# Graph network kernel: type-embedding weight products moved to the prologue, biases awaited where used, normalised tiles stored by the synchronisation engine

## The reference

```python
x = _layernorm(x + _L0_gnn_ref(x, W_fc, attn_l, attn_r, W_res, src, dst))
h = jnp.concatenate([x, node_emb[node_type]], axis=-1)        # 768 + 128
def rgcn_conv(h, src, dst, edge_type, w_rel, w_root, bias):
    xw = jnp.einsum('nd,rde->rne', h, w_rel)                   # one matrix for each of 3 relations
    msg = xw[edge_type, src] * inv[dst, edge_type][:, None]    # mean over the edges of a relation
    return jax.ops.segment_sum(msg, dst, num_nodes) + h @ w_root + bias
h = relu(rgcn_conv(h, ..., w_rel1, w_root1, b1))               # and two more, 896->896->768->768
return _layernorm(x + h)
```

## Time and profile before

| | |
|---|---|
| median of 3 runs | 2536.57 us (2536.53 to 2536.61) |
| profiled execution | 2534.83 us, its span in the trace 2533.0 us |
| PE busy | 2204.2 us, 87% of the span |
| DVE, ACT, POOL busy | 49%, 31%, 18% |
| DMA | mean 85 GB/s |

### The profile page before, as it was taken

The page is one execution under the profiler, slowest core; times in us unless marked ns, Lnnn a source line. Parts: engine busy times, 40 slices in busy tenths (PEclk is TensorE's granted clock), DMA queues, the critical chain, the costliest instruction groups (busy, mean ns, idle before and its releaser), DMA issues.

```text
span 2533.0 us, 29974 instructions
## 1 busy us (share of the span) xinstructions
PE 2204.2 (87%) x10953; PEld 1843.8 (73%) x10954; DVE 1230.3 (49%) x1882; ACT 780.5 (31%) x1062; POOL 450.6 (18%) x378
## 2 busy tenths in 40 slices
PE   3997762778878649999999999999999989999997
PEld 1554441233333239999999989999999989999997
DVE  7887657887786453332232342333232342334335
ACT  0133224676677432121121141121221231212212
POOL 0000002787779610000000000000000000000000
PEclk9999885899889869999999999999999999999999
DMA  0133332211011142333243432333323423434332
GB/s 17 45 85 90 90 88 65 69 31 31 16 31 31 51 145 70 100 109 105 88 117 88 110 105 83 97 93 101 116 79 110 120 84 96 118 106 132 104 99 79
DMA packets 138639, 215.04 MB, mean 85 GB/s; under 512 B 87580, under 2 KB 87818, under 8 KB 138513
## 3 DMA queue, kind: packets, MB, share of 16 engines
q1 hardware_dynamic: 99179, 147.28, 20.3%
q0 software_dynamic: 39344, 66.16, 9.0%
HBM read 182.38 MB, written 30.62 MB: 84 GB/s over the span
## 4 chain that ended last, share of the span: by engine, by line
PE 57%; DMA 5%; DVE 2%; ACT 2%; issue 0%; SPq 0%; ACTq 0%; DVEq 0%
PE banks L1101 29%; PE banks L1073 26%; DMA w_raw<-in_L_gnn_w_root_dram 3%; DVE w_lo L1342 1%; ACT w_hi L1221 1%; DMA s_x<-x_tiles 1%; PE banks L1136 0%; PE banks L1110 0%; DMA emb_raw<-in_L_gnn_w_rel_dram 0%; PE banks L1123 0%; PE banks L1154 0%; DVE h_lo L1373 0%; ACT accT L1249 0%; DVE tail_stats L1392 0%; DVE back L1390 0%
## 5 line engine op out<-in xcount | busy, mean ns | idle before, releaser
L1073 PE MATMUL banks<-ct_in,h_hi 125*128 125x416 f32 (+1 forms) x1710 | 604.5, 353 | 0.6 <-ACT accT L1206 0.6
L1073 PE MATMUL banks<-ct_in,h_lo 125*128 125x416 f32 (+1 forms) x1710 | 603.3, 353 | 0.0
L1101 PE MATMUL banks<-g_hi,w_hi 128*128 128x416 f32 (+1 forms) x1440 | 517.1, 359 | 22.0 <-DVE g_lo L1364 22.0
L1101 PE MATMUL banks<-g_lo,w_hi 128*128 128x416 f32 (+1 forms) x1440 | 513.3, 356 | 0.0
L1101 PE MATMUL banks<-g_hi,w_lo 128*128 128x416 f32 (+1 forms) x1440 | 512.5, 356 | 0.0
L1342 DVE TENSOR_TENSOR w_lo<-w_raw,w_hi 128x768 fp32r<-128x768 f32 (+1 forms) x228 | 227.8, 1000 | 467.3 <-ACT w_hi L1221 467.3
L849 PE MATMUL head_sums<-pw,x 125*65 125x512 f32 x720 | 299.1, 564 | 59.1 <-POOL pw L647 49.2
L1221 ACT CAST w_hi<-w_raw 128x768 fp32r<-128x768 f32 (+1 forms) x228 | 197.8, 868 | 450.1 <-PE banks L1101 354.7
L1073 PEld LDWEIGHTS banks<-ct_in,h_lo 125*128 125x128 f32 x1710 | 323.7, 189 | 4.3
L647 POOL TENSOR_TENSOR pw<-y,csum 125x1250 f32<-125x1250 f32 x120 | 313.6, 2658 | 74.3 <-PE head_sums L849 68.8
L1073 PEld LDWEIGHTS banks<-ct_in,h_hi 125*128 125x128 f32 x1710 | 322.5, 189 | 4.1 <-ACT accT L1206 0.8
(11 more groups left out here) (189 smaller groups left out, 1544.3 us busy)
## 6 DMA issues: line engine op xcount, KB each, us to landing
w_raw<-in_L_gnn_w_rel_dram SPq DMA_DIRECT2D x117, 384.0 KB, 3.1
ct_in<-s_ct POOLq DMA_DIRECT2D x18, 2031.2 KB, 28.4
w_raw<-in_L_gnn_w_rel_dram SPq DMA_DIRECT2D x54, 448.0 KB, 3.9
ct_in<-s_ct POOLq DMA_DIRECT2D x9, 2041.0 KB, 28.6
s_ct<-ct_stage SPq DMA_DIRECT2D x30, 610.4 KB
w_raw<-in_L_gnn_w_root_dram SPq DMA_DIRECT2D x39, 384.0 KB, 3.1
w_raw<-in_L_gnn_w_root_dram SPq DMA_DIRECT2D x18, 448.0 KB, 5.7
low_spread<-s_low SPq DMA_DIRECT2D x12, 610.4 KB
```

What stands on the lines that cost most here:

```text
L1073: ins = nc.tensor.matmul(pb[0:rows, PA, 0:s.w], a, b, start=j == 0, stop=j == len(pairs) - 1)
L1101: ins = nc.tensor.matmul(pb[:, m, 0:s.w], a, b, start=s.first and j == 0, stop=s.last and j == len(parts) - 1)
```

## The change

1. The weight products of the type embedding move from the start of `rgcn_layers` to the prologue of `count_matrices`. ACT issues the four weight loads, PE multiplies in the window buffers, ACT rounds (`emb_split`) and copies three rows (`emb_full`), POOL subtracts in place of DVE, and ACT stores all 67 rows of 3584 numbers to a new array `s_emb` in memory and waits for the store. SP loads them back after the third weight load of `rgcn_layers`.
2. The wait for the biases moves from the start of ACT's and DVE's programs to `output`.
3. The ten stores of `x1` move from POOL to SP, between the weight loads (`X1_STORES`). POOL's second `ct_in` load waits for nothing now.
4. ACT takes a root of a constant at its start (loading the root's table), and the order of the first four tiles on ACT and DVE changes: DVE takes the statistics of tiles 2 and 3 before `h_lo` of tiles 0 and 1, and the first weight splits come after all four tiles.
5. In `attention`, `turn_sums` of head 10 moves between the tiles of head 11; the turning of the embedding on PE and its copies on DVE go.

```diff
@@ count_matrices @@
+            sp.dma_start(emb[:], io["L1_gnn_node_emb"]).then_inc(emb_in, 16)
             sp.dma_start(xs[:], io["x"][0:T, :]).then_inc(x_in, 16)
...
+            for q in range(R + 1):
+                pool.wait_ge(emb_copied, q + 1)
+                nc.gpsimd.tensor_tensor(emb_w[at, q], emb_full[at], emb_w[at, q], ALU.subtract).then_inc(emb_low, 1)
...
         @block.scalar
+            act.wait_ge(raw_in, 48)
+            for q in range(R + 1):
+                rows = io["L1_gnn_w_root1"][D:D1, :] if q == 0 else io["L1_gnn_w_rel1"][q - 1, D:D1, :]
+                act.dma_start(emb_raw[:, q], rows).then_inc(emb_w_in, 16)
...
+            for q in range(R + 1):
+                act.wait_ge(emb_done, q + 1)
+                nc.scalar.copy(emb_w[0:TY, q].bitcast(F32R).rearrange("p (c n) -> p c n", c=2),
+                               win[0:TY, q % 2, :, 0:D1 // 2]).then_inc(emb_high, 1)
+                act.wait_ge(emb_low, q)
+                act.wait_ge(emb_high, q + 1)
+                nc.scalar.copy(emb_full[32:32 + R].rearrange("p (c n) -> p c n", c=2),
+                               win[32:32 + R, q % 2, :, 0:D1 // 2]).then_inc(emb_copied, 1)
+            act.wait_ge(emb_low, R + 1)
+            act.dma_start(dram["emb"].rearrange("p q n -> p (q n)"), emb_w[0:TY].rearrange("p q n -> p (q n)")).then_inc(emb_out, 16)
+            act.wait_ge(emb_out, 16)
             act.wait_ge(consts, 10)
...
@@ attention, PE @@
-            pe.wait_ge(emb_kept, 3)
-            turn_sums(H - 2)
+                if s == 5 and h == H - 1:
+                    turn_sums(h - 1)
             turn_sums(H - 1)
...
+X1_STORES = {1: (0, 1), 2: (2, 3), 4: (4, 5), 6: (6, 7), 8: (8, 9)}
@@ rgcn_layers, SP @@
-            for q in range(R + 1):
-                src = io["L1_gnn_w_root1"][D:D1, :] if q == 0 else io["L1_gnn_w_rel1"][q - 1, D:D1, :]
-                sp.dma_start(emb_raw[:, q], src).then_inc(emb_in, 16)
+            def store_x1(t):
+                sp.wait_ge(normed, t + 1)
+                sp.dma_start(dram["x1"][t * T:(t + 1) * T, :], x1[t % 3]).then_inc(x1_out[t % 3], 16)
...
                 sp.dma_start(w_raw[:, j % 2, 0:s.mt * 128], weights_of(s)).then_inc(w_in[j % 2], 16)
+                if j == 2:
+                    sp.dma_start(emb_w[0:TY].bitcast(F32), dram["emb"]).then_inc(emb_in, 16)
+                if j in X1_STORES:
+                    for t in X1_STORES[j]:
+                        store_x1(t)
@@ rgcn_layers, POOL @@
-                if j == 1:
-                    pool.wait_ge(emb_done, 1)
...
-            for t in range(NT):
-                pool.wait_ge(normed, t + 1)
-                pool.dma_start(dram["x1"][t * T:(t + 1) * T, :], x1[t % 3]).then_inc(x1_out[t % 3], 16)
@@ rgcn_layers, DVE @@
-            dve.wait_ge(bias_in, 48)
-            for p in range(2):
-                for stage in range(4):
-                    first_norm(p, stage)
-                if p == 0:
-                    for q in range(R + 1):
-                        embed(q)
-                    split_w(STEPS[0])
-                    split_w(STEPS[1])
-                for t in (2 * p, 2 * p + 1):
-                    low_h(t)
+            for stage in range(4):
+                first_norm(0, stage)
+            for stage in range(3):
+                first_norm(1, stage)
+            for t in (0, 1):
+                low_h(t)
+            first_norm(1, 3)
+            split_w(STEPS[0])
+            split_w(STEPS[1])
             split_g(STEPS[0])
+            for t in (2, 3):
+                low_h(t)
```

More of the change, by code:

```diff
@@ L53 @@
 A1_K = 2 * H
+KH = D1 // 128
+TY = 64 + R
 ROWS = [(0, 418), (418, 416), (834, 416)]
 def count_matrices(nc, io, dram, csum, nbr, a1_high, a1_low, a2_col, a_rows, under, stored, proj_out, rows_out, ident):
-    stage, csf, xs, xT, res, iota_key, row, rowp, num = under
+    stage, csf, xs, xT, res, iota_key, row, rowp, num, emb_raw, emb_w, emb_full = under
     with ExitStack() as ctx:
@@ L322, in _ @@
         def _(act):
+            act.wait_ge(raw_in, 48)
+            for q in range(R + 1):
+                rows = io["L1_gnn_w_root1"][D:D1, :] if q == 0 else io["L1_gnn_w_rel1"][q - 1, D:D1, :]
+                act.dma_start(emb_raw[:, q], rows).then_inc(emb_w_in, 16)
+            act.wait_ge(emb_turned, 1)
+            act.wait_ge(emb_zero, 1)
+            for c in range(3):
+                nc.scalar.copy(emb_cols[:, c * 32:c * 32 + R], tp[:, 2, 0:R]).then_inc(emb_kept, 1)
+            for q in range(R + 1):
[9 more added lines that the diff above has]
+            act.wait_ge(emb_out, 16)
             act.wait_ge(consts, 10)
@@ L393, in _ @@
                              start=True, stop=True).then_inc(u_sum, 1)
+            pe.wait_ge(emb_in, 16)
+            nc.tensor.transpose(tp[:, 2, 0:R], emb[:], ident[0:R, 0:R]).then_inc(emb_turned, 1)
+            pe.wait_ge(emb_kept, 3)
+            pe.wait_ge(emb_w_in, 16 * (R + 1))
+            for q in range(R + 1):
+                if q >= 2:
+                    pe.wait_ge(emb_copied, q - 1)
+                for c in range(2):
+                    ins = nc.tensor.matmul(win[0:TY, q % 2, c, 0:D1 // 2], emb_cols[:], emb_raw[:, q, c * (D1 // 2):(c + 1) * (D1 // 2)],
+                                           start=True, stop=True)
+                ins.then_inc(emb_done, 1)
+            pe.wait_ge(emb_copied, R + 1)
             pe.wait_ge(u_ready, 4)
@@ L801, in _ @@
             kind_tables()
-            emb_columns()
             divide(H - 2)
@@ L1103, in product @@
                 ins.then_inc(prod_done, 1)
-            def embed():
-                pe.wait_ge(emb_in, 16 * (R + 1))
-                half = D1 // 2
-                for q in range(R + 1):
-                    for c in range(2):
-                        ins = nc.tensor.matmul(pb[0:TY, 2 * q + c, 0:half], emb_cols[:],
-                                               emb_raw[:, q, c * half:(c + 1) * half], start=True, stop=True)
-                ins.then_inc(emb_done, 1)
             def turn_x1(t, c):
@@ L1255, in root_of_chunk @@
                 nc.scalar.activation(ve_b[0:w, c % 4, 1:2], ve_b[0:w, c % 4, 0:1], ACT.Sqrt).then_inc(tail_rooted, 1)
-            act.wait_ge(bias_in, 48)
-            for q in range(R + 1):
-                embed(q)
+            nc.scalar.activation(warm[:], ident[0:T, 0:1], ACT.Sqrt)
             split_w(STEPS[0])
             split_w(STEPS[1])
-            for p in range(2):
-                root_of_variance(p)
-                for t in (2 * p, 2 * p + 1):
-                    keep_h(t)
-                    keep_x1(t, 0)
-                    keep_x1(t, 1)
+            root_of_variance(0)
+            for t in (0, 1):
+                keep_h(t)
+            for t in (0, 1):
+                keep_x1(t, 0)
+                keep_x1(t, 1)
+            root_of_variance(1)
+            for t in (2, 3):
+                keep_x1(t, 0)
+                keep_x1(t, 1)
             split_g(STEPS[0])
+            for t in (2, 3):
+                keep_h(t)
             for s in STEPS:
@@ L1459, in build @@
             under = stage, csf, xs, xT, res_tile, iota_key, row, rowp, num
+        with sb("emb_raw", [128, R + 1, D1], F32) as emb_raw:
+            pass
+        with sb("ct_stage_first", [128, R, NT, T], F32), sb("emb_split", [TY, R + 1, D1], F32) as emb_split:
+            pass
+        with sb("ct_stage_both", [128, 2, R, NT, T], F32), sb("emb_full", [32 + R, D1], F32) as emb_full:
+            under += emb_raw, emb_split, emb_full
         with sb("csum", [128, NT * N], F32) as c, sb("nbr", [128, NT * N], BF16) as m:
```

78 lines of the change are left out of this document (29 added, 49 removed).

## The result

| | before | after |
|---|---|---|
| median of the runs taken side by side, us | 2536.59 (2536.53 to 2542.03, 4 runs) | 2567.06 (2564.29 to 2572.2, 4 runs) |
| profiled execution, us | 2534.83 | 2564.29 |
| its span, us | 2533.0 | 2562.5 |

The change makes the kernel slower: ratio 1.0117 [1.0094, 1.014].

What follows compares the result with a forecast made beforehand. PE was taken as busy nine tenths of nearly every slice from the 16th, waiting at the head, attention's end and first norm. Terms -2 + 9.4 + 17.6 = +25 on 2534.83 gave 2559.8; forecast 2560, range 2540 to 2574.

Steps and rivals of the forecast that it cites:

- Attention, -2: Attention's end: PE's first turn, moved four tiles earlier, is nearly covered; gain 2 us (0.5 to 3.6).
- POOL against DVE, +6.9: Prologue: DVE waits out POOL's four subtractions during `oh_rem`, adding 6.9 us to its chain to the table (below, 0).
- Weights late for DVE, +1: Prologue: four weight loads share the DMA engines with loads DVE waits for at 12.83; +1 us (0 to 2.5).
- The table's transfer behind the store, +1.5: Prologue: the window table's small transfer meets the store of `s_emb` in flight; +1.5 us (0 to 3.5).
- The store hidden under the counts, 0: Prologue: the one-engine store, about 30 to 72 us, ends before ACT's copies are needed; cost 0.
- ACT comes too late: Rival, prologue: a store over 51 us on one engine makes PE wait for ACT; 2570 at 61 us; chance 0.07.
- The norm, +17.6: First norm: the 67-row load on one engine delays tile 2's store, so tile 5 waits; +17.6 us (+6 to +24).
- rows spread: Rival: the 67 rows use many engines or hold up nothing behind them; sum -14, 2523 us; chance 0.15.
- The prologue costs nothing: Rival, prologue: DVE does not wait for POOL; sum +15.6, 2552 us; chance 0.2.

Runs made afterwards that it cites:

- split kernels: The changed kernel with the store and the load of the products each made as 64 and 3 rows; 2526.83 us, 0.9962 of before.
- store-split kernel: The changed kernel with only the store of the products made as 64 and 3 rows; 2562.66 us, 1.0106 of before.

## Why the prediction was right

2560 was forecast in 2540 to 2574, and 2567.06 was measured. The forecast was for one engine moving 67 rows, and that is what the split kernels showed: remove it, and 2571.35 becomes 2526.44 with the same work (only the wait that holds POOL goes too; the windows start at 48.39 with it and at 48.04 without). The rate was near as well: the store took 37 us, 26 KB/us, where 40 and 24.1 were taken. For the profiled pair the sum said 2559.8 and the time was 2564.29. The terms missed by -1.6, +3.8 and +2.3, so little of the closeness is errors that cancel. Term by term:

- *Attention, -2:* -3.6. The upper bound was right: the last turn did fall from 3.85 to 2.40. Undone by itself it is 3.9 at the stage's end, of which the time shows little.
- *POOL against DVE, +6.9:* +7.5, and in the way said, whole instructions of one in whole instructions of the other. What no step foresaw is that the outcome isn't fixed: of the eight profiles in which POOL was free to subtract as soon as the copies were there (the changed kernel's among them), three ran in the first way and five in the second, where `oh_rem` keeps its 22.3 us and POOL is the one that waits.
- *Weights late for DVE, +1:* 0 (12.87 against 12.83).
- *The table's transfer behind the store, +1.5:* +6.0. This is the term that was mis-sized, by more than its bound of 3.5. The prediction gave no working for its size; the wait lasted 8.01 us, and 2.00 with the store split.
- *The store hidden under the counts, 0:* true in the first way, in which it is issued at 35.9 and ACT's first copy comes at 79.56. In the second way, it is the rival "ACT comes too late": I gave it 0.07 and 2570, asked for an engine slower than 19 KB/us, and the cause is a store that begins 13.5 us later. Fixed by holding POOL it gives 2571.39. The changed kernel's two longer runs, 2569.77 and 2572.2, fit it; they weren't profiled, so this is inferred.
- *The norm, +17.6:* 22.6 at the first aggregate, 19.9 at the end. "Tile 5 at 946, 74 us after the stage's start", came 79.4 after it. Most of the 5 us is the step before: tile 0's store took 14.87 us, where I had put 10.4, the landing time of weight loads in a stretch with one load of counts. The second load of counts explains only 1.9 of these 4.5 (14.61 against 12.67 in the split kernels); the store is slower than I took it under one load too, and with none tile 3 doesn't wait for it. From there the lengths hold: the load at 905.76, tile 5 at 960.98, 55 us for 960 KB and the store.
- *Rivals:* "rows spread" said 2523 if the load held up nothing. It is not this kernel. With the rows spread by hand the time is 2526.83, near 2523, but by luck: two errors cancel. The head and attention together cost 1.4 us at the norm's start (873.39 against 872.01) where the rival's sum had 7.4, and the norm, to the first aggregate, gains 9.6 (89.5 us against 99.1) where it had 21. The third weights, the 67 rows and tile 2's store, 16 us in its working, took 24 (896.86 to 920.52). "The prologue costs nothing" (2552) is refuted: 13.2 us at the x products.

Still open: the store-split kernel's three runs without profile (2561.41 to 2565.17) are longer than its profiled one in the second way (2557.28). The first way costs 3.6 us more at the windows with a split store; that makes 2561, and the longest is 4 above it. And which moment of POOL's request decides between the two ways: the first requests came at 21.34, 21.59 and 21.96 us in the first way and at 21.98 to 24.05 in the second, next to each other at 21.96 and 21.98.

## What to carry to other kernels

Before you give a queue a new transfer, work out how many DMA engines its row count lets it have, and what is queued behind it: 67 rows as 64 + 3 turned a loss of 30 us into a gain of 9. Saved work counts only where nothing else sets the pace; here 3.9 us saved ahead of a stage paced by transfers left 0.9, while holding back 4 MB that nobody needed yet gave 9 in the time, 7 of them seen in the norm. And before you put a small gain or loss down to your edit, look whether the head of the program ran the same way in both profiles: here that alone moved the stages behind it by some 3 us. And a small operation on GpSimd beside a stretch of VectorE that sets the pace is not small: put it where VectorE waits, or expect its full length on one of the two.

## What the runs showed of the hardware

- *Which of two engines waits is not fixed.* The same instructions on DVE and POOL gave `oh_rem` 29.81 us with POOL's rows at 2.25 to 3.09, or 22.30 with a POOL row of 17.08. Against back-to-back DVE pieces of 1.19 us, one every 1.12, POOL can be kept out for all that are left, even for 8 numbers (16.47 us). The Trainium skill (the section named above) says of VectorE's two-port modes that whoever issues first blocks the other for the whole instruction. `oh_rem`, a two-input instruction, shows the same for one instruction (a piece of 3.08 us instead of 1.19), and the rows go beyond it: POOL was held over more than 14 of DVE's pieces in a row (16.47/1.12), not one.
- *A transfer on one engine slows the others.* The fourth weights, behind it on its queue, landed 36.2 us after their issue in the changed kernel and 25.8 in the split one. The two loads of counts, on POOL's queue, needed 55.4 us beside it and 43.9 beside the split one. (Before, they needed 28, but one came after the other and not both at once.)
- *A pause of PE costs twice.* After 10 us of waiting for ScalarE the same 12 matmuls took 2.93 us at a lower granted clock, and 1.55 where PE hadn't waited.
